# Loading only weight blocks first, first-block passes one chunk apart, and an earlier read of the third sum, in a fused convolution and low-rank kernel on one core

## Chip, cores and metric

The kernel runs on one core of a Trainium2 chip. The metric is the device time of one execution in microseconds (us), as the median of several runs. One execution was also taken with the hardware profiler; all rows shown here are of that one.

## What is computed

The input x has shape 128 x 64 x 1024 (samples, channels, positions). Four residual stages follow one another, each adding its result to x:

```python
x = x + _L0_cond_ref(x, itok_B_8_3872, log_dt, C, log_A_real, A_imag, D)   # masked causal convolution with a state-space kernel
x = x + _L1_cond_ref(x, itok_B_0_15, weights)          # einsum('bct,bcd->bdt', x, weights[condition])
x = x + _L2_cond_ref(x, itok_B_6_15, base_weight, base_bias, lora_A_w, lora_B_w)  # x @ base_weight.T + bias + (x A.T) B.T
x = x + _L3_cond_ref(x, itok_B_0_2, W, lora_A, lora_B_w)  # x @ W.T + 0.5 (x A) B.T
```

Stages 2 and 3 are linear over the 1024 positions, so the kernel first multiplies (base_weight + I) with (W + I) once, and then applies the product to all rows, with the low-rank terms beside it. All arithmetic is float32 with 32-bit sums; matrix products of full precision are made of three passes over a high and a low part of each operand (high x high, high x low, low x high).

## The kernel before

The program is written engine by engine with semaphores. There is no scheduler: on each engine the order is the order of the code. It has three phases.

**Setup (0 to about 179 us).** The SP queue loads the eight 512 KB blocks of W (`w3_raw`, L898) and the eight 512 KB blocks of base_weight (`p2`, L895), and after them the low-rank tables `a3raw`, `b2raw`, `b2raw3` (L909 to L911). Between the first blocks it also loads three small tensors for the convolution kernel (L903) and stores a block of zeros (L906). The ACT queue issues seven more small loads before any of its work (L1111). For each of the eight chunks of W, VectorE adds the identity to the diagonal block (`w3_identity`, L1282), ScalarE makes the high part (`p3[.., 0, ..]`, L1158, semaphore `p3_hi`), and VectorE makes the low part (`p3_low`, L1286, `p3_lo`). The first block of base_weight (`p2[0]`) is split in the same way into `staged[0]`: its high part on ScalarE (L1126, `staged_hi`), its low part on VectorE (L1297, `staged_lo`). The second block (`p2[4]`) gets its identity from GpSimd (L1057), its high part from ScalarE and its low part from VectorE (L1303).

TensorE first runs 20 multiplications by the identity (`keep_clock`, L409), which only keep it busy. Then it computes the product of the first block, the job `d0`, chunk by chunk (L1640 to L1647): for each chunk c of the contraction three passes (a, b), where a picks the high or low part of the staged block and b that of p3; each pass is two multiplications of 512 columns. The job `d4` follows (L1664), then small products with the low-rank table (`a3a`, `a3b`, L1611), and between them four transposes of the parameters of the convolution kernel (`parameters`, L1650 to L1656). The transposes wait for `base_ready`, which VectorE raises at the end of a serial chain of small operations (L1307 to L1373); within the chain it waits for the seven small loads (`in_later`, L1355). The job `a3b` waits until VectorE has copied the transposed parameters (`part_ready`, L1444). The rest of the setup is further products of blocks.

**Convolution (about 179 to 547 us).** For each of the 64 channels TensorE multiplies by a Toeplitz matrix (`convolve`, L1715 to L1748); a hardware loop (`Fori`) runs over groups of eight channels.

**Dense phase (about 547 us to the end).** 32 pairs of samples, one pass of `pair(n, last_one)` for each. Pair 0 and pair 31 are straight code, pairs 1 to 30 are a hardware loop, so that a branch back is taken after pairs 1 to 29. For each pair TensorE computes seven Strassen-like products (L802 to L818), applies low-rank terms (`low_rank`, L825), and, for the next pair, does four quarters of the stage-1 mixing (`quarter`, L787). At the end of a pair's code TensorE has, in this order: the product M7 into the bank `of_p` (`m7_done`), the low-rank terms of the second sample (`v_done`), quarter 3 of the next pair, a wait for `u3_read`, and the last low-rank term into `of_p` (`p_done`). `u3_read` is raised by VectorE once it has read the third sum out of `of_p` (L765), which it may do after `m7_done`. The next pair's code opens with `wide_product` of xa11 (L808, L809 alternating).

VectorE's part at the same place, before the change:

```python
            if not last_one:
                h_low(dve, n + 1, 1)
                sums(n + 1)                      # L680, L681, L684
            dve.wait_ge(m7_done, n + 1)
            tt(y_out[1][:, 0:HB], y_out[1][:, 0:HB], of_p, ALU.add).then_inc(u3_read, 1)   # L765
```

`sums(n + 1)` adds two quarters (L680), makes the low part of xa22 (L681), then waits for ScalarE's high part of that sum (`s1_hi`, L581) and makes the low part xs1 (L684, `s1_lo`), which TensorE needs for the second product of the next pair.

## Time and profile before

| what | value |
|---|---|
| median of 3 runs | 1442.49 us (1442.35 to 1443.65) |
| the profiled execution's own time | 1442.2 us |
| span of its profile | 1440.3 us |
| TensorE (PE) busy | 1430.6 us, 99% of the span |
| VectorE (DVE) busy | 1127.9 us, 78% |
| ScalarE (ACT) busy | 611.8 us, 42% |
| GpSimd (POOL) busy | 101.0 us, 7% |
| moved by DMA | 272.98 MB, mean 190 GB/s |

Times of rows are counted from the start of the span; the profiled execution's own time is 1.9 us more than its span. PE is the matrix multiplications of TensorE, PEld its weight loads, which may run ahead of the multiplications. A matrix multiplication is shown from the start to its modelled end, so neighbours overlap, and a float32 multiplication appears as two records. "Idle before" is how long the engine did nothing ahead of a row, and what ended it.

### The profile page before, as it was taken

How to read it: one execution, taken by the hardware profiler on the slowest of the kernel's cores; microseconds unless marked ns; L12 is line 12 of the kernel's file. 1: busy time of each engine (PE TensorE's matmuls, PEld its weight loads, DVE VectorE, ACT ScalarE, POOL GpSimd, SP SyncE). 2: the span in 40 equal slices, each digit the busy share in tenths (PEclk: the TensorE clock that was granted, in tenths of full speed). 3: DMA queues.
4: the chain of work that ended last, by engine and by line, in shares of the span. 5: the costliest groups of instructions: out<-in, count | busy, mean ns of one | idle time of the engine just before them, and what ended most of it. 6: DMA issues, size and time to landing. Idle time of an engine off the chain costs nothing.

```text
span 1440.3 us, 31112 instructions
## 1 busy us (share of the span) xinstructions
PE 1430.6 (99%) x9274; PEld 1319.5 (92%) x9274; DVE 1127.9 (78%) x2256; ACT 611.8 (42%) x1217; POOL 101.0 (7%) x187
## 2 busy tenths in 40 slices
PE   9999999999999999999999999999999999999999
PEld 7888899999999998999999999999999999999998
DVE  7985398888888887777887787787788788778775
ACT  4331276566656663333433432333343343233332
POOL 2322100000000001000000000000000000000000
PEclk9999999999999999999999999999999999999999
DMA  8032288888888787555565565566556555555642
GB/s 315 1 132 77 59 284 275 272 275 273 275 274 275 271 270 205 189 184 156 176 187 153 171 188 161 154 188 186 155 175 188 156 167 190 160 155 188 185 154 82
DMA packets 117451, 272.98 MB, mean 190 GB/s; under 512 B 24300, under 2 KB 60527, under 8 KB 114759
## 3 DMA queue, kind: packets, MB, share of 16 engines
q1 hardware_dynamic: 107366, 238.91, 53.9%
q10 hardware_dynamic: 10054, 33.68, 5.8%
q8 instruction: 17, 0.28, 0.1%
q14 instruction: 14, 0.11, 0.0%
HBM read 199.60 MB, written 72.88 MB: 189 GB/s over the span
## 4 chain that ended last, share of the span: by engine, by line
PE 98%; DMA 1%; DVE 0%; SPq 0%; issue 0%; DVEq 0%
PE ps L816 18%; PE ps L809 17%; PE ps L1735 14%; PE ps L808 13%; PE ps L787 8%; PE ps L1625 7%; PE ps L1746 6%; PE ps L825 4%; PE ps L1726 3%; PE ps L1611 2%; PE ps L1738 2%; PE ps L1646 1%; PE ps L1634 1%; PE ps L1664 1%; DMA w_raw<-in_L_cond_W 1%; PE ps L800 0%
## 5 line engine op out<-in xcount | busy, mean ns | idle before, releaser
L808 PE MATMUL ps<-weights,xa 128*128 128x256 f32 x1152 | 322.6, 283 | 0.7
L809 PE MATMUL ps<-weights,xa 128*128 128x352 f32 x1152 | 322.2, 321 | 0.0
L816 PE MATMUL ps<-weights,xs 128*128 128x512 f32 x1152 | 292.1, 401 | 0.0
L816 PEld LDWEIGHTS ps<-weights,xs 128*128 128x128 f32 x1152 | 207.1, 189 | 41.3
L574 ACT ACTIVATE a<-ps 128x512 f32<-128x512 f32 x128 | 76.5, 598 | 375.4 <-PE ps L787 375.4
L808 PEld LDWEIGHTS ps<-weights,xa 128*128 128x128 f32 x1152 | 216.8, 188 | 12.4 <-issue 12.3
L1735 PE MATMUL ps<-toep,ut 128*128 128x512 f32 (+2 forms) x1152 | 226.8, 342 | 0.0
L809 PEld LDWEIGHTS ps<-weights,xa 128*128 128x128 f32 x1152 | 216.4, 188 | 0.1
L1735 PEld LDWEIGHTS ps<-toep,ut 128*128 128x128 f32 x1152 | 194.3, 189 | 16.6
L787 PEld LDWEIGHTS ps<-m_gath,x_in 128*128 128x128 f32 x1024 | 130.9, 191 | 7.6 <-DVE x_in L672 2.3
L787 PE MATMUL ps<-m_gath,x_in 128*128 128x128 f32 x1024 | 135.0, 275 | 1.9 <-DVE x_in L672 1.9
L1217 ACT ACTIVATE ut<-xt 128x896 fp32r<-128x896 f32 x64 | 61.0, 954 | 138.3 <-PE ps L1746 129.7
L809 PE MATMUL ps<-weights,xs 128*128 128x352 f32 x384 | 107.7, 322 | 0.0
L662 DVE COPY_PREDICATED x_in<-late,x_nat 128x512 f32<-128x512 uint16 x124 | 92.7, 748 | 18.9 <-DVE late L657 18.7
L1746 PE MATMUL ps<-toep,ut 128*128 128x256 f32 x768 | 107.3, 289 | 0.0
L808 PE MATMUL ps<-weights,xs 128*128 128x256 f32 x384 | 106.4, 280 | 0.0
L384 POOL COPY m_gath<-mix 64x64 f32 x128 | 50.3, 393 | 786.0 <-PE ps L787 709.1
L1625 PE MATMUL ps<-p,staged 128*128 128x512 f32 x432 | 98.8, 390 | 0.0
L1625 PEld LDWEIGHTS ps<-p,staged 128*128 128x128 f32 x432 | 80.9, 188 | 17.9 <-issue 1.1
L1746 PEld LDWEIGHTS ps<-toep,ut 128*128 128x128 f32 x768 | 95.8, 190 | 0.0
L692 DVE COPY hrow<-ps 64x48 f32<-64x48 f32 x128 | 26.3, 205 | 75.1 <-PE ps L809 74.2
L461 ACT ACTIVATE weights<-tab 128x128 fp32r<-128x128 f32 (+1 forms) x256 | 71.6, 353 | 29.4 <-DVE tab L468 29.4
(233 smaller groups left out, 2251.1 us busy)
## 6 DMA issues: line engine op xcount, KB each, us to landing
xt<-in_xt SPq DMA_DIRECT2D x64, 512.0 KB, 5.6
x_d<-yo SPq DMA_DIRECT2D x64, 512.0 KB, 2.9
x_nat<-in_x SPq DMA_DIRECT2D x64, 512.0 KB, 4.2
lags<-kern_d SPq DMA_DIRECT2D x63, 512.0 KB, 4.9
x_in<-x_d SPq DMA_DIRECT2D x62, 512.0 KB
out<-y_out ACTq DMA_DIRECT2D x62, 512.0 KB, 5.3
stack<-b_d SPq DMA_DIRECT2D x130, 128.0 KB, 4.2
tab<-a_d SPq DMA_DIRECT2D x128, 128.0 KB, 2.1
```

The source lines that it names most:

```text
L461: ins = nc.scalar.activation(to, of, ACT.Copy)
L574: ins = copy(raw[:], mixing, ACT.Copy)
L662: nc.vector.copy_predicated(x1_in[v][:, cols], late[:], x_nat[v][:, cols]).then_inc(chosen[v], 1)
L787: ins = mm(acc[:, bank, i * P:(i + 1) * P], x1_in[v][:, c * P:(c + 1) * P], m_gath[v][:], start=True, stop=True)
L808: mm(acc[:, left, 0:HALF], x_part, w[:, 0:HALF], start=start, stop=end, skip_group_check=True)
L809: ins = mm(acc[:, right, 0:HALF + KR], x_part, w[:, HALF:WIDE], start=start, stop=end, skip_group_check=True)
L816: ins = mm(acc[:, bank], operand[:, a, i, :], plain(i, b, m), start=opens and i == a == b == 0, stop=i == K4 - 1 and a == 1, skip_group_ch ...
L825: ins = mm(piece, hs[v][0:rows, j, :], stack[v][0:rows, j, at_col:at_col + width], start=False, stop=j == 1, skip_group_check=True)
L1217: copy(ut[u % 2][:, 0, 0:SPLIT], xt[u % BUFS][:, 0:SPLIT], ACT.Copy).then_inc(ut_hi, 1)
L1625: ins = mm(t[:, cols], staged[n % 2][:, a, c, :], p3[:, c, b, cols], start=c == a == b == 0, stop=c == K8 - 1 and a == 1)
L1735: mm(y[:, half * HB + i * P:(half + 1) * HB], xs[:, a, half * half_t + i, :], tp[:, b, 0:HB - i * P], start=i == a == b == 0, stop=False)
L1746: ins = mm(y[:, to:to + QT], xs[:, a, i, :], tp[:, b, at_col:at_col + QT], start=False, stop=i == half_t - 1 and a == 1)
```

## The change

Three places change. The three small loads of the SP queue and the store of zeros move behind the eight blocks of W (and ahead of `p2[4]`); the seven small loads of the ACT queue move behind ScalarE's last piece of the first two blocks. On TensorE the first pass of chunk c + 1 comes ahead of the second and third pass of chunk c. On VectorE the last third of `sums` becomes `s1_low`, and the read of the third sum (`third`) stands ahead of it.

```diff
@@ VectorE, dense phase
             tt(s1[:], a21[:], a22[:], ALU.add).then_inc(s1_raw, 1)
             tt(xa22[:, 1], a22[:], f(xa22[:, 0]), ALU.subtract).then_inc(a22_lo, 1)
+
+        def third(n):
+            dve.wait_ge(m7_done, n + 1)
+            tt(y_out[1][:, 0:HB], y_out[1][:, 0:HB], of_p, ALU.add).then_inc(u3_read, 1)
+
+        def s1_low(n):
             dve.wait_ge(s1_hi, n + 1)
             dve.wait_ge(s1_raw, n + 1)
             tt(xs1[:, 1], s1[:], f(xs1[:, 0]), ALU.subtract).then_inc(s1_lo, 1)
@@
         sums(0)
+        s1_low(0)
@@
                 sums(n + 1)
-            dve.wait_ge(m7_done, n + 1)
-            tt(y_out[1][:, 0:HB], y_out[1][:, 0:HB], of_p, ALU.add).then_inc(u3_read, 1)
+            third(n)
+            if not last_one:
+                s1_low(n + 1)
@@ SP queue
                     load_p2(p2[0], 0, in_w2[0])
-                if i == 1:
-                    for to, of in ((logs[:, 0:N], log_a_real), (logs[:, N:N + 1], log_dt.unsqueeze(1)), (aim[:], a_imag)):
-                        sp.dma_start(to, of).then_inc(in_small, 16)
-                if i == 2:
-                    sp.wait_ge(consts, 7)
-                    sp.dma_start(kern_d[:, T:T + P], zero[:]).then_inc(kern_stored, 16)
+            for to, of in ((logs[:, 0:N], log_a_real), (logs[:, N:N + 1], log_dt.unsqueeze(1)), (aim[:], a_imag)):
+                sp.dma_start(to, of).then_inc(in_small, 16)
+            sp.wait_ge(consts, 7)
+            sp.dma_start(kern_d[:, T:T + P], zero[:]).then_inc(kern_stored, 16)
             for i in BLOCKS[1:]:
                 load_p2(p2[i], i, in_w2[i])
@@ ACT queue: the loop of seven loads (cri, steps_all, dcol, bias_col, index x3) moves
-            for to, of in (...):
-                act.dma_start(to, of).then_inc(in_later, 16)
...
             stage_high(1)
+            for to, of in (...):
+                act.dma_start(to, of).then_inc(in_later, 16)
             act.wait_ge(trig_in, 1)
@@ TensorE, job d0
+            def first_pass(c, a, b):
+                pe.wait_ge((p3_hi, p3_lo)[b], c + 1)
+                pe.wait_ge((staged_hi, staged_lo)[a], 1)
+                for half in range(2):
+                    cols = slice(half * HB, (half + 1) * HB)
+                    ins = mm(target("d0")[:, cols], staged[0][:, a, c, :], p3[:, c, b, cols],
+                             start=c == a == b == 0, stop=c == K8 - 1 and b == 1)
+                return ins
+
+            first_pass(0, 0, 0)
             for c in range(K8):
-                for a, b in ((0, 0), (1, 0), (0, 1)):
...
+                if c + 1 < K8:
+                    first_pass(c + 1, 0, 0)
+                first_pass(c, 1, 0)
+                ins = first_pass(c, 0, 1)
             ins.then_inc(job_done, 1)
```

TensorE's order at the start of job d0 before the change (the semaphores that a row waits for stand behind it; a row without them is the second half of its pass):

```order
L1646 MATMUL ps<-p_72,staged_73 128x512 [waits staged_hi,p3_hi]
L1646 MATMUL ps<-p_72,staged_73 128x512
L1646 MATMUL ps<-p_72,staged_73 128x512 [waits staged_lo,p3_hi]
L1646 MATMUL ps<-p_72,staged_73 128x512
L1646 MATMUL ps<-p_72,staged_73 128x512 [waits staged_hi,p3_lo]
```

and the same place after it, with numbers in the names (line 1650 is in `first_pass`):

```order
L1650 MATMUL ps<-p3_72,staged0_73 128x512 [waits staged_hi,p3_hi]
L1650 MATMUL ps<-p3_72,staged0_73 128x512
L1650 MATMUL ps<-p3_72,staged0_73 128x512 [waits staged_hi,p3_hi]
L1650 MATMUL ps<-p3_72,staged0_73 128x512
L1650 MATMUL ps<-p3_72,staged0_73 128x512 [waits staged_lo,p3_hi]
L1650 MATMUL ps<-p3_72,staged0_73 128x512
L1650 MATMUL ps<-p3_72,staged0_73 128x512 [waits staged_hi,p3_lo]
```

A second pass that needs only high parts, that of chunk 1, now stands between the first pass of chunk 0 and the two passes of chunk 0 that need a low part.

VectorE's order at the end of a pair of the loop, before:

```order
L680 TENSOR_TENSOR s_170<-a_167,a_168 128x512 [waits quarter_read]
L681 TENSOR_TENSOR xa_159<-a_168,xa_159 128x512
L684 TENSOR_TENSOR xs_157<-s_170,xs_157 128x512 [waits x_s1_raw,x_s1_hi]
L765 TENSOR_TENSOR y_out_172<-y_out_172,ps 128x512 [waits m7_done]
L768 TENSOR_TENSOR y_out_172<-y_out_172,ps 128x512 [waits u3_read,v_done]
L770 TENSOR_TENSOR y_out_172<-y_out_172,ps 128x512 [waits p_done]
```

and after (L685 is the old L765, L690 the old L684):

```order
L680 TENSOR_TENSOR s_170<-a_167,a_168 128x512 [waits quarter_read]
L681 TENSOR_TENSOR xa_159<-a_168,xa_159 128x512
L685 TENSOR_TENSOR y_out_172<-y_out_172,ps 128x512 [waits m7_done]
L690 TENSOR_TENSOR xs_157<-s_170,xs_157 128x512 [waits x_s1_raw,x_s1_hi]
L776 TENSOR_TENSOR y_out_172<-y_out_172,ps 128x512 [waits u3_read,v_done]
L778 TENSOR_TENSOR y_out_172<-y_out_172,ps 128x512 [waits p_done]
```

The read of the third sum and the low part of xs1 have changed places; nothing else moved there.

## Rows read from the trace of the kernel before

**Rows 1.** The page, busy time of each engine over the span.

```profile
PE 1430.6 (99%) x9274; PEld 1319.5 (92%) x9274; DVE 1127.9 (78%) x2256; ACT 611.8 (42%) x1217; POOL 101.0 (7%) x187
```

**Rows 2.** Waits of TensorE's weight loads, whole span: total us, times, longest us.

```profile
PEld ps L808 <- issue: 12.3, 29, 0.5
...
PEld ps L1655 <- DVE lens_cols L1373: 0.3, 1, 0.3
```

**Rows 3.** Timeline of TensorE, start: start us, us, instruction, count, idle before.

```profile
1.57 6.80 PE L409 MATMUL ps<-ident 128*128 128x128 f32 x40 [1.57 <-POOL ident L1021]
8.13 0.70 PE L1646 MATMUL ps<-p,staged 128*128 128x512 f32 x2
10.69 10.99 PE L1646 MATMUL ps<-p,staged 128*128 128x512 f32 x46 [1.85 <-DVE staged L1297]
21.51 11.04 PE L1664 MATMUL ps<-p,staged 128*128 128x512 f32 x48
...
43.46 0.46 PE L1655 MATMUL ps<-ident,par 64*128 64x64 f32 x4
```

**Rows 4.** Timeline of VectorE, the start and its serial chain.

```profile
5.63 0.29 DVE L1293 TENSOR_TENSOR p<-p,ident 128x128 f32<-128x128 f32 x1 [1.18 <-DMA p<-in_L_cond_base_weight]
...
9.11 0.29 DVE L1282 TENSOR_TENSOR w_raw<-w_raw,ident 128x128 f32<-128x128 f32 x1 [0.82 <-DMA w_raw<-in_L_cond_W]
...
11.21 0.29 DVE L1282 TENSOR_TENSOR w_raw<-w_raw,ident 128x128 f32<-128x128 f32 x1 [0.67 <-DMA w_raw<-in_L_cond_W]
...
17.95 0.28 DVE L1282 TENSOR_TENSOR w_raw<-w_raw,ident 128x128 f32<-128x128 f32 x1
...
34.49 2.26 DVE L1345 TENSOR_TENSOR n<-n,n 64x64 f32<-64x64 f32 x1
...
37.37 1.70 DVE L1347 TENSOR_TENSOR n<-n,aim 64x64 f32<-64x64 f32 x1
...
40.87 0.22 DVE L1363 COPY par<-n 64x128 f32<-64x128 f32 x1
```

**Rows 5.** Stretches: length, busy us of PE to POOL, clock, DMA share, GB/s.

```profile
5.00:6.50 1.50, 1.50 (x11) 1.50 (x11) 0.29 (x1) 1.49 (x2) 0.11 (x1) 1.00 0.34 59
...
11.00:19.00 8.00, 8.00 (x35) 6.21 (x34) 7.79 (x12) 6.04 (x6) 0.00 (x0) 1.00 1.03 415
```

**Rows 6.** Timeline of GpSimd: the second block, and beside VectorE's chain.

```profile
19.12 0.57 POOL L1057 TENSOR_TENSOR p<-p,ident 128x128 f32<-128x128 f32 x1 [14.01 <-DMA p<-in_L_cond_base_weight]
...
34.26 4.73 POOL L1053 TENSOR_TENSOR staged<-b2raw,staged 128x1024 fp32r<-128x1024 f32 x2 [6.53 <-ACT staged L1126]
```

**Rows 7.** Timeline of TensorE, end of pair 17, in the loop.

```profile
1047.85 2.99 PE L816 MATMUL ps<-weights,xs 128*128 128x512 f32 x12
...
1051.99 0.72 PE L825 MATMUL ps<-stack,hs 128*128 128x512 f32 x2
...
1052.90 0.32 PE L809 MATMUL ps<-weights,xa 128*128 128x352 f32 x1
```

**Rows 8.** Timeline of TensorE, end of pair 30, which no branch back follows.

```profile
1412.03 0.72 PE L825 MATMUL ps<-stack,hs 128*128 128x512 f32 x2
...
1412.70 0.32 PE L809 MATMUL ps<-weights,xa 128*128 128x352 f32 x1
```

**Rows 9.** Timeline of TensorE in the convolution: first and last of 64 channels.

```profile
179.11 0.88 PE L1726 MATMUL ps<-toep,dt 128*128 128x256 f32 x6
...
541.57 0.88 PE L1726 MATMUL ps<-toep,dt 128*128 128x256 f32 x6
```

**Rows 10.** Timeline of VectorE, end of pair 17.

```profile
1051.26 0.68 DVE L765 TENSOR_TENSOR y_out<-y_out,ps 128x512 f32<-128x512 f32 x1
```

**Rows 11.** Timeline of TensorE's weight loads, end of pair 1.

```profile
609.24 0.30 PEld L825 LDWEIGHTS ps<-stack,hs 128*128 128x128 f32 x2 [0.22 <-DVE y_out L765]
610.05 0.19 PEld L808 LDWEIGHTS ps<-weights,xa 128*128 128x128 f32 x1 [0.52 <-issue]
```

**Rows 12.** DMA issues of the first 60 us: size, median us to landing.

```profile
b2raw<-in_L_cond_lora_B_w SPq DMA_DIRECT2D x1, 512.0 KB, 19.8
```

More of the change, by code:

```diff
@@ L1104, in trig @@
                 nc.scalar.activation(to, to, ACT.Sin, scale=scale, bias=bias).then_inc(fac_sin, 1)
-            for to, of in ((cri[:], ssm_c.rearrange("h n c -> h (n c)")), (steps_all[:], steps.unsqueeze(0).to_broadcast([P, B])),
-                           (dcol[:], ssm_d.unsqueeze(0).to_broadcast([G, C])),
-                           (bias_col[:], bias2),
-                           (index[:, 0:B], cond.unsqueeze(0)), (index[:, B:2 * B], adapter.unsqueeze(0)),
-                           (index[:, 2 * B:3 * B], labeler.unsqueeze(0))):
-                act.dma_start(to, of).then_inc(in_later, 16)
             def stage_high(n):
@@ L1161, in _ @@
             stage_high(1)
+            for to, of in ((cri[:], ssm_c.rearrange("h n c -> h (n c)")), (steps_all[:], steps.unsqueeze(0).to_broadcast([P, B])),
+                           (dcol[:], ssm_d.unsqueeze(0).to_broadcast([G, C])),
+                           (bias_col[:], bias2),
+                           (index[:, 0:B], cond.unsqueeze(0)), (index[:, B:2 * B], adapter.unsqueeze(0)),
+                           (index[:, 2 * B:3 * B], labeler.unsqueeze(0))):
+                act.dma_start(to, of).then_inc(in_later, 16)
             act.wait_ge(trig_in, 1)
@@ L1639, in _ @@
             keep_clock(target("a3a"), FILL_START)
-            for c in range(K8):
-                for a, b in ((0, 0), (1, 0), (0, 1)):
-                    pe.wait_ge((p3_hi, p3_lo)[b], c + 1)
-                    pe.wait_ge((staged_hi, staged_lo)[a], 1)
-                    for half in range(2):
-                        cols = slice(half * HB, (half + 1) * HB)
-                        ins = mm(target("d0")[:, cols], staged[0][:, a, c, :], p3[:, c, b, cols],
-                                 start=c == a == b == 0, stop=c == K8 - 1 and b == 1)
+            def first_pass(c, a, b):
[7 more added lines that the diff above has]
+            first_pass(0, 0, 0)
+            for c in range(K8):
+                if c + 1 < K8:
+                    first_pass(c + 1, 0, 0)
+                first_pass(c, 1, 0)
+                ins = first_pass(c, 0, 1)
             ins.then_inc(job_done, 1)
```

## The prediction

> **What bounds the kernel now.** I read the page first: TensorE is busy for 99% of the span and VectorE for 78% [rows 1]. So only what makes TensorE stand, or start late, can change the time. Three views show where it stands: the waits of its weight loads [rows 2], its timeline at the start [rows 3], and its timeline where one pair of the dense phase ends and the next begins [rows 7, 8]. There are two kinds of place.
>
> At the start TensorE multiplies by the identity until 1.57 + 6.80 = 8.37 us, does one pass of d0, then stands for 1.85 us until the low part of the first block is made [rows 3]. From then on it is fed, except at the parameters: their weight load waits 0.3 us for VectorE [rows 2], so VectorE's chain and TensorE arrive together at 43.46.
>
> In the dense phase the weight load of L808 stands 12.3 us in all, 29 times, put down to "issue" [rows 2]: once for each of the 29 branches back. What it costs the multiplications is read from two ends of pairs. Where the branch follows, the first L809 starts 52.90 - 51.99 = 0.91 us after the last low-rank term [rows 7]; where straight code follows it is 12.70 - 12.03 = 0.67 [rows 8]. That stall is among the smaller: in pair 1 the load stood 0.52 us [rows 11]. The mean stall is 12.3 / 29 = 0.42. The load of pair 17 comes 0.69 us after L825 and stood about 0.39 (L825's two loads take 0.30), for a cost of 0.24, so 0.15 of a stall is hidden, and the mean cost is 0.27 us.
>
> Does a branch by itself cost that? In the convolution, a loop with seven trips round eight channels, 63 steps from channel to channel take 541.57 - 179.11 = 362.46 us, or 5.753 each [rows 9], and no step differs from the next by over 0.01 in the timeline. There the branch is free: no wait that ends late stands near it. In the dense loop one does: `u3_read` stands right before the last two multiplications, and VectorE reads the third sum from 1051.26 to 1051.94, after which L825 starts at 1051.99 [rows 7, 10]. I take it that the issuing side stands at that wait, and only afterwards can issue the last term, branch, and fetch and issue the next pair's code.
>
> **The change part by part.**
>
> *Order of loads.* Nothing is added; eleven small DMAs move. The first blocks of W and base_weight have landed by 5.63, the next block of W only by 9.11 [rows 4], and between 5.0 and 6.5 the DMA engines move 59 GB/s against 415 later [rows 5]: the small loads hold the block up. A 512 KB block at 415 GB/s takes 1.26 us. With only blocks in the queues the third lands at about 5.63 + 1.26 = 6.9; VectorE makes the low part of chunk 0 first; ScalarE's high part of it no longer stands behind seven issues, so that work too is done at about 7.1, and VectorE takes the block then. So VectorE's whole row of work moves by 9.11 - 7.1 = 2.0 us. If the gap in the transfers stays for another reason, the block lands at 8.0 and it moves by 1.1. The three SP loads and the store of zeros now stand ahead of `p2[4]`, as they did; it landed at 19.1 [rows 6] and moves forward with the rest, to about 17 to 18. ScalarE's seven issues come after the high part of that block, when ScalarE would only wait for VectorE, so I cost them at nothing; what uncovers that is a rival below.
>
> *Passes of d0.* The first pass of chunk 1 fills the place where TensorE stood 1.85 us. Its 48 multiplications run at the pace of d4, 11.04 / 48 = 0.23 us [rows 3], so from 8.13 they end at 19.2 instead of 21.51: 2.3 us sooner. For this the high part of chunk c + 1 must be there at 8.8 + 1.38 c; VectorE took a new diagonal block every (17.95 - 11.21) / 5 = 1.35 us [rows 4], a little less than the 1.38 that six multiplications take, and ScalarE's part follows each within some 1.3 us: 8.4 for chunk 1, where 8.8 is needed, and no step later than that. With the block at 8.0 TensorE loses another 0.6.
>
> *What is late next.* TensorE would be at the parameters at 43.46 - 2.3 = 41.1. VectorE's chain starts 2.0 us sooner, but it meets GpSimd's two operations of 2.4 us each, beginning at 34.26 [rows 6]. Two operations of VectorE that otherwise take 0.22 lasted 2.26 and 1.70 beside them: 3.5 us lost [rows 4]. In the new order GpSimd finds VectorE some eight operations further on, past the reciprocal that ran beside it, so I expect 4.2 us lost. The chain then ends at 43.4 - 2.0 + 0.7 = 42.1 and TensorE waits there one us. The copy that `a3b` waits for hangs on the same chain and moves with it. **The start gives 43.4 - 42.1 = 1.3 us.** Bounds: 2.0 (no additional time lost to GpSimd) and 0.6 (block at 8.0). After that TensorE's work is in turn what the other engines wait for, and its stretches have no stall, so the gain is carried to the end.
>
> *The third sum.* M7 ends at 1047.85 + 2.99 = 1050.84 [rows 7], and VectorE, which now reads the sum before making the low part of xs1, can begin at about 1050.88 in place of 1051.26 [rows 10]: `u3_read` comes 0.38 us sooner. A load of L808 that stood 0.42 us on average then stands 0.04, and the longest stands 0.14, below the 0.15 that is hidden. **29 x 0.27 = 7.8 us.** Bounds: nothing (the branch is not held by this wait) and 7.8 plus the few hundredths by which L825 itself may come sooner, at most 28 x 0.02 = 0.6. In pairs 0 and 1 VectorE is later than in the others and L825 itself waits, 0.22 us in pair 1 [rows 11] and less in pair 0: another 0.3. The low part of xs1 comes 0.7 us later, at 1052.1; its product follows 24 multiplications after 1052.7, over 3 us later, so that cover holds. In the last pair nothing stood ahead of the read, and nothing changes.
>
> **Sum:** 1.3 + 7.8 + 0.3 = 9.4 us off the profiled execution's 1442.2, so 1432.8; the median of the runs is 0.3 higher, so **1433.0** rounded.
>
> **The rivals.**
>
> *The branch is not held by the wait.* The issuing side might put the waiting multiplication in a queue and read on; then the 0.4 us are the price of the branch whatever VectorE does, and the change gives 1.3 + 0.3: 1440.6. Against it stand the convolution's free branches [rows 9], and pair 1: its L825 came 0.22 us late, and the next load followed 0.81 us after it, not sooner than the 0.69 of pair 17 [rows 11, 7], so the delay was passed on rather than absorbed. For it: I see the issuing side in no row, and 0.81 beside 0.69 is also in the spread from pair to pair. The Trainium skill speaks for this rival ("Advanced Engine Details and Errata", Sequencer Loop): an engine instruction is pushed into the engine's queue, waits for its semaphores there, and further ones are read meanwhile. By that rule the third part gives 0.3 us instead of 8.1. I give it 0.2.
>
> *Half of it.* The wait holds the branch, but freed 0.38 us earlier the issuing side still has to wait for room, and half of each stall stays: 3.9 in place of 7.8, so 1436.7. I give it 0.13.
>
> *The seven loads come late.* They are issued from about 19 to 23 us, while big loads fill the DMA engines; the last of these took 19.8 us to land [rows 12]. If the small ones took 20.2 from the last issue, VectorE would get them at 43.6, where it needed them at 40.87 [rows 4], and the chain would end 2.7 us later than before. With a branch that the wait does not hold, the time is 1442.2 + 2.7 - 0.3 = 1444.6, and more with each further us of landing. It decides from a landing at 40.9. Against it: the big loads are all down by about 35 us, and what is issued beside them should not take longer. I give it 0.03.
>
> **How the numbers follow.** My forecast has 0.62: 1431.2 to 1435.0, from 1.3 widened to 0.6 to 2.0 at the start, and 7.0 to 8.4 at the branches. The half has 0.13, the rule's case 0.2, the late loads 0.03, and 0.02 is left for what I do not see. The range reaches from the low end of my own case to the rule's case: **1431.2 to 1441.0**. A change of 0.2% (2.9 us) is about what a measurement of this kernel can tell from none. My case and the half are faster by more: 0.75. The rule's case, 1.6 us, is within it: with the rest, 0.22. Slower by more: 0.03.
>
> **What would show it.** In the changed kernel's profile d0's 48 multiplications run from 8.1 without a stall and d4 starts near 19.2; the second W block's diagonal is made near 7.1; the parameters start near 42.1, with their load waiting about 1 us for VectorE. In the waits the row of L808's loads put down to issue shrinks from 12.3 us to under 4; ends of pairs in the loop have L809 about 0.67 us after L825; the step from pair to pair is shorter by 0.27 us. If that row stays at 12 us I am wrong about what holds the branch; if L1655 starts at 43.4 again, the start gave nothing.

## The result and the profile after

| | before | after |
|---|---|---|
| median of 6 runs each | 1442.42 us (1442.22 to 1443.65) | 1430.62 us (1429.81 to 1432.42) |
| ratio, with its 95% interval | | 0.9919 (0.9906 to 0.9932) |
| the profiled execution's own time | 1442.2 us | 1431.91 us |
| span of its profile | 1440.3 us | 1430.0 us |

The kernel is 11.8 us faster by the medians and 10.3 us by the two profiled executions. Forecast were 9.4 us and 1433.0, with 1431.2 as the low end: direction and place were right, the sum was too small, and the result lies 0.6 us below the range.

**Page.** Busy time of each engine over the span, after:

```profile
PE 1421.1 (99%) x9274; PEld 1318.3 (92%) x9274; DVE 1124.2 (79%) x2256; ACT 612.4 (43%) x1217; POOL 106.7 (7%) x187
```

The counts are those of [rows 1]: no work was removed. The matrix multiplications' busy time fell by 9.5 us, although the weight loads' fell by only 1.2, because the timeline leaves no gap between multiplications there: in before, at the end of pair 17, L825 is drawn from 1051.99 to 1052.71 and L808 from 1052.68, although the load between them stood 0.39 us. So a share of 99% said little about how much could be gained, before and after.

**Waits of TensorE's weight loads,** after (total us, times, longest us):

```profile
PEld ps L795 <- DVE x_in L672: 3.5, 2, 2.9
...
PEld ps L816 <- issue: 1.4, 6, 0.4
...
PEld ps L1667 <- DVE lens_cols L1378: 0.9, 1, 0.9
```

The row of 12.3 us, 29 times [rows 2] has become 1.4 us, 6 times (the old L808 is L816). The row counts only stalls above 0.15 us. With the smaller ones these 29 loads stood 2.9 us in the trace, at least 0.04 each, which is also what the one at the end of pair 30 has, where no branch follows. The wait at the parameters has grown from 0.3 to 0.9 us, as forecast. The largest is now one at the entry of the dense phase; it had stood second in the list of before as well:

```profile
PEld ps L787 <- DVE x_in L672: 2.3, 2, 1.9
```

**End of pair 17,** timeline of TensorE's multiplications after (start us, us, instruction, count):

```profile
1042.26 3.00 PE L824 MATMUL ps<-weights,xs 128*128 128x512 f32 x12
1045.09 0.64 PE L833 MATMUL ps<-stack,hs 128*128 128x256 f32 x4
1045.56 1.06 PE L795 MATMUL ps<-m_gath,x_in 128*128 128x128 f32 x8
1046.37 0.71 PE L833 MATMUL ps<-stack,hs 128*128 128x512 f32 x2
1046.93 0.28 PE L816 MATMUL ps<-weights,xa 128*128 128x256 f32 x1
1047.04 0.33 PE L817 MATMUL ps<-weights,xa 128*128 128x352 f32 x1
```

and VectorE at the same place:

```profile
1045.29 0.69 DVE L685 TENSOR_TENSOR y_out<-y_out,ps 128x512 f32<-128x512 f32 x1 [0.34 <-PE ps L824]
1045.89 0.69 DVE L690 TENSOR_TENSOR xs<-s,xs 128x512 fp32r<-128x512 f32 x1
```

VectorE now waits for M7, reads the third sum from 1045.29 to 1045.98, and only then makes the low part of xs1. L833 (the old L825) starts at 1046.37, so 0.39 us after the read; before, it started 0.05 us after it [rows 7, 10]. The first L817 follows L833 by 1047.04 - 1046.37 = 0.67 us, the distance that straight code had [rows 8]. Over all pairs of the loop that distance was 0.85 to 1.04 us before and is 0.66 to 0.70 now, with one exception: pair 1, where it is 0.93. The timeline of the weight loads shows that one:

```profile
608.84 0.30 PEld L833 LDWEIGHTS ps<-stack,hs 128*128 128x128 f32 x2
609.55 0.19 PEld L816 LDWEIGHTS ps<-weights,xa 128*128 128x128 f32 x1 [0.41 <-issue]
```

VectorE's timeline shows why this one is left:

```profile
608.11 0.68 DVE L685 TENSOR_TENSOR y_out<-y_out,ps 128x512 f32<-128x512 f32 x1
```

The read did not wait for M7 here, as in pair 17; it followed VectorE's earlier work without a gap and ended at 608.79, 0.05 us before L833. So in pair 1 the wait still ended late, and its stall stayed. In `third_alone` and `pool_waits`, two kernels described below, VectorE was in time in pair 1 too: the read ended 0.40 us ahead of L833, and the first L817 came 0.66 and 0.67 us after it.

**The issuing side in the trace.** The timeline does not draw what an engine's sequencer does, but the view of one line does (PEldq is TensorE's sequencer, L374 is the loop; the numbers are the shortest, median and longest duration in ns, and the start). The branch back at the end of pair 17, before:

```profile
L374 PEldq COMPARE_BRANCH  x1: 215/215/215, 1052.1 to 1052.1; - x1
```

and after:

```profile
L374 PEldq COMPARE_BRANCH  x1: 208/208/208, 1046.1 to 1046.1; - x1
```

In the trace's finer times it starts 0.15 us after the end of VectorE's read (1051.94 and 1045.98), in each of the 29 taken branches of before and of after. Where TensorE's own work stands makes no difference to it: in before it starts 0.10 us after the last low-rank term, in after 0.25 us ahead of it, while quarter 3 still runs. A taken branch lasts 0.21 to 0.22 us. The first load of the next trip then starts 0.78 us after the end of the read on average in before (0.69 to 0.87), and 0.76 in after (0.71 to 0.86). So the issuing side does stand at the wait for `u3_read`, and from there the next trip's first load takes much the same stretch in both kernels, about 0.8 us. What of this stretch TensorE's last work does not cover is the stall.

**Start,** timeline of TensorE after:

```profile
1.57 6.99 PE L409 MATMUL ps<-ident 128*128 128x128 f32 x40 [1.57 <-POOL ident L1027]
8.32 11.43 PE L1650 MATMUL ps<-p,staged 128*128 128x512 f32 x48
19.63 11.17 PE L1676 MATMUL ps<-p,staged 128*128 128x512 f32 x48
30.64 11.03 PE L1616 MATMUL ps<-a3raw,p 128*128 128x160 f32 x80
42.37 0.46 PE L1667 MATMUL ps<-ident,par 64*128 64x64 f32 x4 [0.70 <-DVE lens_cols L1378]
```

d0 runs without a stall and d4 starts at 19.63 instead of 21.51 [rows 3]. The parameters start at 42.37 instead of 43.46, after a wait for VectorE: 1.1 us, where 1.3 were forecast. What the DMA engines did between 5.0 and 6.5 us (length, busy us of PE to POOL, clock, DMA share, GB/s):

```profile
5.00:6.50 1.50, 1.50 (x9) 1.50 (x9) 1.19 (x2) 1.42 (x2) 0.11 (x1) 1.00 0.95 358
```

They moved 358 GB/s instead of 59 [rows 5], so the gap in the transfers was the small loads' doing. Which of the two queues' loads did it was not separated. Still the next block of W was not taken at 7.1 as forecast but at 7.49, as VectorE's timeline shows:

```profile
5.31 0.29 DVE L1298 TENSOR_TENSOR p<-p,ident 128x128 f32<-128x128 f32 x1 [0.85 <-DMA p<-in_L_cond_base_weight]
5.58 1.23 DVE L1291 TENSOR_TENSOR p<-w_raw,p 128x1024 fp32r<-128x1024 f32 x1
7.49 0.29 DVE L1287 TENSOR_TENSOR w_raw<-w_raw,ident 128x128 f32<-128x128 f32 x1 [0.69 <-DMA w_raw<-in_L_cond_W]
7.70 1.22 DVE L1302 TENSOR_TENSOR staged<-p,staged 128x1024 fp32r<-128x1024 f32 x1
...
15.73 2.44 DVE L1291 TENSOR_TENSOR p<-w_raw,p 128x1024 fp32r<-128x1024 f32 x2
19.61 1.35 DVE L1308 TENSOR_TENSOR staged<-p,staged 128x1024 fp32r<-128x1024 f32 x1 [1.45 <-ACT staged L1125]
...
33.79 2.13 DVE L1352 TENSOR_TENSOR n<-n,aim 64x64 f32<-64x64 f32 x1
35.96 2.28 DVE L1353 TENSOR_TENSOR n<-n,exps 64x64 f32<-64x64 f32 x1
```

The low part that d0 needs (L1302) now runs from 7.70 to 8.92, where before TensorE had to wait for it until 10.69 [rows 3]. Beside GpSimd's work two operations of VectorE took 2.13 and 2.28 us instead of 0.22: 4.0 us lost, where 4.2 were forecast and 3.5 had been lost before. New is the idle time of 1.45 us ahead of L1308, at 19.61. The timeline of GpSimd and that of ScalarE show where it comes from:

```profile
16.95 1.54 POOL L1063 TENSOR_TENSOR p<-p,ident 128x128 f32<-128x128 f32 x1 [11.82 <-DMA p<-in_L_cond_base_weight]
```

```profile
18.52 1.06 ACT L1125 ACTIVATE staged<-p 128x1024 fp32r<-128x1024 f32 x1 [1.61 <-POOL p L1063]
```

The second block now lands at 16.95 instead of 19.12 [rows 6]. But GpSimd's addition of the identity, which took 0.57 us there, takes 1.54 now. ScalarE has to wait 1.61 us for it, and VectorE waits for ScalarE. It ends at 18.49, 0.32 us after VectorE's last two low parts of W, which end at 15.73 + 2.44 = 18.17. The nine profiles with moved loads fall into two kinds. In five (both of after among them) the addition took 1.16 to 1.54 us and ended 0.31 to 0.32 us after VectorE's pair, and the parameters started at 42.25 to 43.47. In the other four it took 0.46 us, VectorE's pair took 2.67 to 2.74 instead of 2.44 or 2.45, and the parameters started at 41.79 to 42.80. So one of the two holds the other, and which it is hangs on the moment at which the block lands. VectorE's second operation of the pair starts about 1.21 us after its first. In the four, GpSimd's addition started 1.12 to 1.20 us after the pair's start, so just ahead of that second operation; in the five, 1.21 to 1.60 us after it.

**Where the 10.3 us of the profile lie.** For both kernels I took TensorE's timeline and split each of the 30 steps from pair to pair at the first multiplication of every group. The means, in us; the other eleven groups together differ by less than 0.01:

| segment | before | after | times 30 |
|---|---|---|---|
| last low-rank term to the next pair's first multiplication | 0.717 | 0.553 | 4.9 |
| M1, the 24 weight loads behind it | 3.427 | 3.313 | 3.4 |
| quarter 3 to the last low-rank term | 0.840 | 0.812 | 0.8 |
| M5 | 3.320 | 3.301 | 0.6 |
| M2 and M4 | 6.664 | 6.641 | 0.7 |
| whole step | 27.681 | 27.340 | 10.2 |

So all of it lies in the dense phase. The 1.1 us of the start are not in the profiled execution's total, because both kernels start the dense phase at 550.52 us. After was there sooner, but its first quarter waited for a part of x that comes back from memory:

```profile
PE ps L795 <- DVE x_in L672: 3.1, 2, 2.8
```

In before and in the eleven other profiles of this study the longest wait of this row was between 0.6 and 2.3 us. What the start gives therefore shows in the medians and not in this one execution; its own time is also 1.3 us above the median of after. Over all profiles of this study it is seen at this place too: the dense phase starts at 548.2 to 550.5 us in the nine with moved loads (mean 549.4) and at 550.5 to 552.7 in the four without (mean 551.4).

### The profile page after: what moved, and what is told of

Its sections match the earlier page's. It is cut to its first block, busy times and chain, and to the rows that moved or that the text cites. A ratio compares the mean times of both kernels' runs of the same rounds, so it can differ in the third digit from the quotient of the medians.

```text
span 1430.0 us, 31112 instructions
## 1 busy us (share of the span) xinstructions
PE 1421.1 (99%) x9274; PEld 1318.3 (92%) x9274; DVE 1124.2 (79%) x2256; ACT 612.4 (43%) x1217; POOL 106.7 (7%) x187
## 4 chain that ended last, share of the span: by engine, by line
PE 96%; DVE 2%; DMA 1%; SPq 1%; issue 0%; POOL 0%; ACT 0%; DVEq 0%; POOLq 0%
PE ps L824 19%; PE ps L817 17%; PE ps L1747 14%; PE ps L816 13%; PE ps L795 8%; PE ps L1630 7%; PE ps L1758 6%; PE ps L833 4%; PE ps L1738 3%; PE ps L1750 2%; PE ps L1616 1%; PE ps L1639 1%; DMA p<-in_L_cond_base_weight 1%; PE ps L808 0%; DMA x_in<-yo 0%; SPq L906 0%
## 5 line engine op out<-in xcount | busy, mean ns | idle before, releaser
L817 PE MATMUL ps<-weights,xa 128*128 128x352 f32 x1152 | 321.0, 322 | 0.0
L816 PE MATMUL ps<-weights,xa 128*128 128x256 f32 x1152 | 318.5, 279 | 0.0
L816 PEld LDWEIGHTS ps<-weights,xa 128*128 128x128 f32 x1152 | 217.0, 188 | 3.0 <-issue 1.4
L817 PEld LDWEIGHTS ps<-weights,xa 128*128 128x128 f32 x1152 | 216.1, 188 | 0.6
L384 POOL COPY m_gath<-mix 64x64 f32 x128 | 56.1, 439 | 772.2 <-PE ps L795 693.6
L817 PE MATMUL ps<-weights,xs 128*128 128x352 f32 x384 | 107.2, 321 | 0.0
L816 PE MATMUL ps<-weights,xs 128*128 128x256 f32 x384 | 105.9, 279 | 0.0
```

The lines of the kernel that those rows point to most:

```text
L816: mm(acc[:, left, 0:HALF], x_part, w[:, 0:HALF], start=start, stop=end, skip_group_check=True)
L817: ins = mm(acc[:, right, 0:HALF + KR], x_part, w[:, HALF:WIDE], start=start, stop=end, skip_group_check=True)
```

## The experiments

Two theories stood against each other. **Held:** the issuing side of TensorE stands at `u3_read` before it can issue the last term and branch back. **Not held:** the branch costs 0.4 us whatever VectorE does. For the start the question was which of the two edits gives anything. Each kernel of a batch was timed beside runs of before on the same chip; those had medians of 1442.75, 1442.39 and 1443.39 us in the three batches. The ratios are of these comparisons and can differ from the quotient of two medians by some 0.0005.

### One part alone

`third_alone` is before with only VectorE's edit:

```diff
+            third(n)
+            if not last_one:
+                s1_low(n + 1)
-            dve.wait_ge(m7_done, n + 1)
-            tt(y_out[1][:, 0:HB], ...).then_inc(u3_read, 1)
```

> The kernel before, with only VectorE's read of the third sum moved ahead of the low part of xs1. Theory A (the branch back is held by the wait for u3_read): the stall of L808's weight load falls from 12.3 us to under 2, a step from pair to pair goes from 27.68 to 27.34 us, as in the changed kernel, and the time falls by 10 to 10.6 us (ratio 0.9928), although the start is untouched. Rival B (the branch is not held, the gain of the changed kernel comes from a different start): 0 to 1 us. Rival C (each part needs the others): between, 3 to 8 us.

Measured: 1433.08 us, ratio 0.9929 (0.9915 to 0.9942). Its list of waits is headed by the start's:

```profile
PEld ps L1654 <- ACT p L1166: 2.4, 1, 2.4
...
PEld ps L816 <- issue: 1.6, 9, 0.2
```

and the stall behind the branch is as small as in after; the step from pair to pair is 27.323 us. This edit alone is worth 9.7 us by the medians and 10.2 by the ratio, most of the whole. A branch that costs the same whatever VectorE does cannot give that.

`loads_alone` is before with only the small loads moved:

```diff
-                if i == 1:
-                    ... logs, logs, aim
-                if i == 2:
-                    ... kern_d
+            ... logs, logs, aim, kern_d      (behind the eight blocks of W)
-            ... seven loads of the ACT queue
             stage_high(1)
+            ... seven loads of the ACT queue
```

> The kernel before, with only the small loads moved behind the weight blocks. My theory: the second W block lands near 7.5 in place of 9.1, the chain of VectorE ends at 42.3 in place of 43.4, the first low part is ready at 8.9 so TensorE stands only some 0.5 us after its filling, and the parameters start at 42.4, where VectorE's chain is what is waited for. Gain at 43.46: 1.1 us, with or without the new order of passes. Rival (the passes are needed for it): under 0.5 us.

Measured: 1441.11 us, ratio 0.999 (0.9981 to 0.9999). Two rows of it, TensorE's timeline at the start and the wait behind the branch:

```profile
8.58 11.52 PE L1643 MATMUL ps<-p,staged 128*128 128x512 f32 x48
```

```profile
PEld ps L808 <- issue: 11.9, 29, 0.5
```

The stall behind the branch is untouched. But d0 already runs without its gap, in the old order of passes.

`passes_alone` is before with only the order of the passes of d0:

```diff
+            first_pass(0, 0, 0)
             for c in range(K8):
+                if c + 1 < K8:
+                    first_pass(c + 1, 0, 0)
+                first_pass(c, 1, 0)
+                ins = first_pass(c, 0, 1)
```

> The kernel before, with only the passes of d0 one chunk apart. The second pass of TensorE would need the high part of chunk 1, made at 9.4 to 10.5 from the block that lands at 9.1, so TensorE stands as long as before, and VectorE's chain still ends at 43.4: no change within 0.2 us. If the order of passes were worth something by itself, d4 would start before 21.3.

Measured: 1442.43 us, ratio 0.9995 (0.9986 to 1.0004), no difference. The first pass of chunk 1 has nothing to work on while the block is late; it waits 1.77 us for ScalarE's part of that block, and another pass 0.35 us:

```profile
10.59 1.74 PE L1645 MATMUL ps<-p,staged 128*128 128x512 f32 x6 [1.77 <-ACT p L1158]
```

In this profile the parameters start at 45.01, where I had expected 43.4 to 43.5. `third_alone`, with the start of before unchanged, has 44.77, so the spread between executions reaches as far, and no price of the passes can be read from it.

`loads_and_passes` is after without VectorE's edit (both diffs above).

> The changed kernel without the early read of the third sum. My theory: as loads_alone, 1.1 us off at the parameters; d4 starts at 19.6, but that is lost again while TensorE waits for VectorE's chain. L808's stall stays near 12.3 us and the step from pair to pair at 27.68. Time 1441.3. Rival (the passes keep what they gain): another 0.5 us or more below loads_alone.

Measured: 1440.82 us, ratio 0.9984 (0.9975 to 0.9994). In its profile the parameters start at 41.83 and the step is 27.703 us, as before. Beside `loads_alone` the difference is 0.3 us, within both intervals.

`no_passes` is after with the old order of the passes (the diff of `passes_alone` the other way round).

> The changed kernel with the old order of passes in d0. If the passes are worth nothing by themselves, as VectorE's chain is what is waited for at the parameters, the time is that of the changed kernel within 0.5 us (1430.6) and the parameters start near 42.4. If they are worth what they gain in d0, it is slower by 0.5 us or more.

Measured: 1432.23 us, ratio 0.9919 (0.9905 to 0.9932), the same ratio as after. Its d0 has a gap of 0.34 us:

```profile
9.62 10.69 PE L1651 MATMUL ps<-p,staged 128*128 128x512 f32 x46 [0.34 <-DVE staged L1302]
```

So in this execution the order of the passes had 0.3 us left to fill, and even that is lost in the wait at the parameters. They start at 43.47, where I had expected 42.4. The ratio alone could not show 0.3 us: its interval is 1.9 us to either side.

`after_again` is after, unchanged, for one more profile.

> The changed kernel once more, unchanged, for a second profile: the dense phase takes the same time from its first product to the end within 0.5 us, and what differs between the two executions lies in the landing of the W block (7.5 in the first) and in the wait for the last rows before the dense phase (2.8 us in the first, 1.7 in the kernel before). Expected: a shorter wait there, 1 to 2 us, and a span 1 us below 1430.0.

Measured: one time, 1431.95 us. Its start differs from that of the first profile:

```profile
9.56 10.81 PE L1650 MATMUL ps<-p,staged 128*128 128x512 f32 x46 [0.50 <-ACT p L1157]
...
43.44 0.46 PE L1667 MATMUL ps<-ident,par 64*128 64x64 f32 x4 [1.14 <-DVE lens_cols L1378]
```

Here the parameters start at 43.44, no sooner than before, because the second W block was taken at 8.12 instead of 7.49. The step (27.346 us) repeats; the row of the stall reads 2.5 us, 12 times, since more of the small stalls are above 0.15 us (with all of them 3.6 us beside 2.9). Over the nine profiles with moved loads the block was taken between 7.49 and 8.31 and the parameters started between 41.79 and 43.47; in the four without, 9.11 to 9.22 and 43.46 to 45.01. The start's gain is a spread: on average the parameters start at 42.5 in the nine and 44.2 in the four, 1.7 us apart, while the profile from which I forecast 1.3 was the earliest of the four.

### Is it the wait or the branch?

`third_after_v` is after with one wait more: VectorE may read the third sum only after `v_done`, which TensorE raises just before quarter 3. The place in VectorE's order stays that of after.

```diff
         def third(n):
             dve.wait_ge(m7_done, n + 1)
+            dve.wait_ge(v_done, n + 1)
```

> The changed kernel, order of VectorE unchanged, but its read of the third sum also waits for v_done, so that u3_read comes some 0.5 us later than in the changed kernel (about 0.1 later than before the change). Theory A (time of u3_read holds the branch): L808's stall is back at 12 us or more, L825's successor starts late, the gain of the third part is gone: 10 to 14 us slower than the changed kernel, 1441 to 1445. Rival B (what helped is that the low part of xs1 comes after the read, not when the read ends): the time stays within 2 us of the changed kernel.

Measured: 1448.34 us, ratio 1.0034 (1.0021 to 1.0046). Its wait behind the branch:

```profile
PEld ps L817 <- issue: 12.2, 29, 0.5
```

The stall is back at its old size, although everything else of the change is in. The kernel lost 17.7 us to after, more than I had expected, because L834 itself now waits as well: quarter 3 to the last term takes 1.012 us instead of 0.812, 6.0 us over 30 pairs. The stall takes (0.715 + 3.408) - (0.553 + 3.313) = 0.257 per pair, 7.7 us. M2 with M4 has (6.730 - 6.641) x 30 = 2.7 of the rest, and 1.2 us more lie in pair 0. VectorE's read and L834 at the end of a pair show the wait with no slack again, as in before:

```profile
1055.17 0.69 DVE L686 TENSOR_TENSOR y_out<-y_out,ps 128x512 f32<-128x512 f32 x1 [0.88 <-PE ps L834]
```

```profile
1055.91 0.73 PE L834 MATMUL ps<-stack,hs 128*128 128x512 f32 x2
```

The read ends at 1055.86 and L834 starts 0.05 us after it. The branch back again starts 0.15 us after the read, in all 29 places.

`third_dose` is after with two fills of 64 columns of unused PSUM before the read. They compute nothing that is used, and make `u3_read` later by a little:

```diff
             dve.wait_ge(m7_done, n + 1)
+            for i in range(2):
+                nc.vector.memset(acc[:, SMALL_BANK, (2 + i) * P:(2 + i) * P + 64], 0.0)
             tt(y_out[1][:, 0:HB], ...).then_inc(u3_read, 1)
```

> The changed kernel, with two small fills of unused columns of the sums' memory on VectorE between its wait for m7_done and its read of the third sum, so that u3_read comes some 0.2 to 0.3 us later than in the changed kernel and still before the place where the kernel before had it (0.4 later). They compute nothing that is used. Theory A with the hidden part: each 0.1 us of delay adds 0.1 us to the weight load of L808 once it is past what is hidden, so its stall reads 4 to 8 us in all where the changed kernel has 1.4 and the kernel before 12.3, and the time is 0.5 to 4 us above the changed kernel. A step (all or nothing) would give either 1.4 or 12.

Measured: 1434.2 us, ratio 0.9934 (0.992 to 0.9947). VectorE at the end of pair 17, and the wait behind the branch:

```profile
1046.45 0.19 DVE L686 MEMSET ps<- 128x64 f32 x2 [0.39 <-PE ps L826]
1046.55 0.67 DVE L687 TENSOR_TENSOR y_out<-y_out,ps 128x512 f32<-128x512 f32 x1
```

```profile
PEld ps L818 <- issue: 6.4, 23, 0.5
```

```profile
L374 PEldq COMPARE_BRANCH  x1: 208/208/208, 1047.4 to 1047.4; - x1
```

The read ends at 1047.22, and L835 starts at 1047.49: 0.27 us later, where before it was 0.05 and in after 0.39. These values line up with the stalls: 0.05 and 12.3 us in before, 0.05 and 12.2 in `third_after_v`, 0.27 and 6.4 here, 0.39 and 1.4 in after. The last term to L819 takes 0.75 us on average over the 31 ends of pairs, between the 0.93 of before and the 0.68 of after. It is no mixture of full stalls and none: outside pair 1 every branch of this kernel has a stall of 0.14 to 0.32 us, where before has 0.34 to 0.52 and after 0.04 to 0.19. The branch starts 0.15 us after the read here too. So the stall is graded by how late the wait ends, and a slack of about 0.4 us is what makes it nearly go away. By the ratios this kernel is 2.2 us slower than after, though the two intervals overlap. This also answers the rival in which half of the stall stays: with the slack whole, L817 follows L833 as in straight code.

`before_two_pairs` keeps everything of before, but TensorE's loop has 15 trips of two pairs, so half of the branches are gone:

```diff
-        over_pairs(pe, pair)
+        pair(0, False)
+        with pe.Fori(1, PAIRS // 2) as k:
+            pair(2 * k - 1, False)
+            pair(2 * k, False)
+        pair(PAIRS - 1, True)
```

> The kernel before, with TensorE's loop over pairs 1 to 30 written as 15 trips of two pairs, so half of its branches back are gone; all else, VectorE's order too, unchanged. Theory A (the stall is the branch held behind a late wait): the stall of L808 appears 14 or 15 times, 6 us in place of 12.3, and the time falls by 4 to 5 us. Rival D (the stall comes from the late wait alone, with or without a branch): 29 stalls, no change. Rival B (a branch costs 0.4 us whatever the wait): the same halving as theory A, told apart from it by the next run.

Measured: 1439.5 us, ratio 0.9977 (0.9966 to 0.9987). The wait, and two ends of pairs that follow each other, without a branch and with one:

```profile
PEld ps L808 <- issue: 7.4, 14, 0.7
```

```profile
1050.82 0.73 PE L825 MATMUL ps<-stack,hs 128*128 128x512 f32 x2
1051.39 0.28 PE L808 MATMUL ps<-weights,xa 128*128 128x256 f32 x1
...
1078.16 0.72 PE L825 MATMUL ps<-stack,hs 128*128 128x512 f32 x2
1078.94 0.38 PE L808 MATMUL ps<-weights,xa 128*128 128x256 f32 x1
```

Of the 31 ends of pairs 17 have L809 0.67 to 0.69 us after L825, the other 14 have 0.95 to 1.17. So a late wait without a branch behind it makes no stall. The 14 stalls are longer than before (7.4 / 14 = 0.53 us instead of 0.42), which is why only 3 us were gained and not the 4 to 5 that I had expected. The additional 0.1 us lies behind the branch: from its end to the first load it is 0.52 us on average here and 0.41 in before. Why a loop body of twice the length makes this longer stays open.

`after_two_pairs` is the same edit on after.

> The changed kernel with the same 15 trips of two pairs on TensorE. Theory A: hardly a stall is left to halve (1.4 us in 6 places), so under 0.7 us faster. Rival B (each branch costs by itself): the gain of before_two_pairs shows again, 4 to 5 us.

Measured: 1431.65 us, ratio 0.9919 (0.9906 to 0.9933): no difference from after, and a step of 27.353. Where the wait ends in time, fewer branches gain nothing. Late wait and branch are both needed for the full stall, and taking either away removes most or all of it. The longer body shows here as well: with the same slack of 0.40 us its row reads 2.5 us, 10 times, and behind some of its 14 branches L817 comes 0.74 to 0.83 us after L833.

### The wait that is left at the start

`pool_waits` is after, with GpSimd's two operations of the chain's time held back until the chain is done:

```diff
+            pool.wait_ge(base_ready, 1)
             stage_low(2)
             stage_low(3)
```

> The changed kernel, with GpSimd waiting for base_ready before its two low parts of 2.4 us each. My theory: they no longer stop VectorE's two operations (2.1 and 2.3 us where 0.2 is usual), VectorE's chain ends near 38.2 in place of 42.3, TensorE no longer waits 0.7 us at the parameters, which then start at 41.7, and the time falls by 0.7 us. GpSimd's parts are done by 43, long before TensorE's b2_0 at 51. Rival (VectorE's stretched operations are not GpSimd's doing): chain still ends at 42.3, no change.

Measured: 1430.55 us, ratio 0.9911 (0.9898 to 0.9925). VectorE's reciprocal and the two operations behind it, and the end of its chain:

```profile
34.01 0.55 DVE L1352 RECIPROCAL n<-n 64x64 f32<-64x64 f32 x1
34.59 0.22 DVE L1353 TENSOR_TENSOR n<-n,aim 64x64 f32<-64x64 f32 x1
34.84 0.22 DVE L1354 TENSOR_TENSOR n<-n,exps 64x64 f32<-64x64 f32 x1
...
38.74 0.39 DVE L1379 CAST lens_cols<-steps_all 64x64 f32<-64x64 int32 x2
```

The operations that lasted 2.13 and 2.28 us take 0.22 each, the chain ends at 39.1 instead of 42.3, and TensorE no longer waits at the parameters. It starts them at 42.25, though, since in this execution its own work got there no sooner: d0 had lost 0.63 us waiting for ScalarE. The time cannot be told from that of after. Its interval reaches furthest down of all kernels here, but I would not claim a gain over after.

## Where the prediction was right, and the step that failed

**Order of loads.** The mechanism was right: the gap in the transfers went (59 to 358 GB/s) and the block came earlier. It was mis-sized: taken at 7.1, measured 7.49 to 8.31 over nine profiles, so my bound of 8.0 is nearer to the truth than my value. I had timed a 512 KB block at the full 415 GB/s in queues that hold only blocks. After's window shows 358, by which the block takes 1.46 us; what makes up the rest of the delay stays open.

**Passes of d0.** I wrote that they fill the 1.85 us and did not ask what they would be worth without the loads, or the loads without them. The runs say: the passes alone nothing (0.9995), their absence from after nothing (0.9919 beside 0.9919). Once the block comes at 7.5 to 8.3, VectorE's low part is ready at 8.9 to 9.7 and the stall is 0.0 to 0.6 us in either order. The 2.3 us that the paragraph on the passes counts are the loads' doing.

**What is late next.** Right in kind: VectorE's chain takes over as the bound, the loss to GpSimd came to 4.0 us (forecast 4.2), and the wait at the parameters was 0.70 us on the multiplications (forecast one). What I missed is the other direction: GpSimd's small addition at 16.95 was slowed itself, 1.54 us instead of 0.57, and cost the chain 1.45 us. Its ends 0.3 us behind VectorE's pair in five profiles speak for a hold by VectorE, and the longer pair in the other four for a short hold by GpSimd; no run took either away. The Trainium skill's page "SBUF — State Buffer" (Who interferes with whom) has both: an operation of VectorE with two inputs in SBUF and one of GpSimd that reads SBUF hold each other up, and which one loses is decided by which was issued first. `pool_waits` agrees for the first direction, with 2.13 and 2.28 us against 0.22; the second is only read from those rows.

**The start as a whole.** Forecast 1.3 us, in bounds of 0.6 to 2.0. The two kernels without VectorE's edit give 1.4 us (ratio 0.999) and 2.3 us (ratio 0.9984), each with an interval of about 1.4 us to either side. The after of the profile had 1.1 at the parameters, and lost it again at the entry of the dense phase. "The gain is carried to the end" was argued too quickly: the wait for x_in at 550 us, the second largest row of before's waits, takes up or gives back about a microsecond from one execution to the next, and the prediction did not price it. In the sum of the medians, 11.8 us less the 10.2 of the dense phase leave 1.6 for the start.

**The third sum.** The reason was right, and it was the step that carried the forecast. `third_alone` shows the gain, `third_after_v` brings the stall back, `third_dose` grades it, and the two kernels with two pairs per trip show that it takes both the late wait and the branch. The issuing side, which the prediction saw in no row, is in the trace: its branch starts 0.15 us after VectorE's read in all eleven profiles with one pair per trip. The rival of the branch that is not held, with its 0.2, is refuted. So is the half, with its 0.13. The convolution, whose branches the prediction took as free, bears it out: its six taken branches last 0.21 to 0.24 us each, and its steps are all 5.75 us long. The seven late loads never happened: in no profile did the chain wait for them. (Its own sum gives 23 + 20.2 = 43.2 for their landing, not 43.6.)

The Trainium skill's rule ("Advanced Engine Details and Errata", Sequencer Loop) says that an instruction is pushed into its engine's queue and waits for its semaphores there, and that other ones can be read and queued while a control instruction is being executed. The prediction read it as letting the issuing side go past a wait. The trace does not agree with that at this place: the branch, which stands behind two multiplications that wait for `u3_read`, starts 0.15 us after the read, whether that is before or behind TensorE's start on them. It does agree in that the issuing side runs ahead of multiplications that wait for nothing but the engine: in after, 0.25 us ahead of L833.

**The step that failed is the size of the sum for the dense phase,** a main term a little too small and two further terms put at nothing. I forecast 7.8 + 0.3 = 8.1 us there and measured 10.2:

| term | forecast | measured (table of segments) |
|---|---|---|
| stalls behind the branch | 29 x 0.27 = 7.8 | 4.9 + 3.4 = 8.3 |
| pair 1's own wait | 0.3 | 0.3 |
| L825 itself sooner in the other pairs | 0, bound 0.6 | 0.8 - 0.3 = 0.5 |
| M5, and M2 with M4 | not priced | 0.6 + 0.7 = 1.3 |

The four measured terms come to 10.4; the other eleven groups give 0.2 back. The main term was good to 0.5 us, although one stall fewer than counted went away (that of pair 1): the other 28 were worth 8.3 / 28 = 0.30 us each, not 0.27. L825 started within 0.05 us of the end of VectorE's read in before, which meant that it was itself held a little in every pair; I saw that, bounded it at 0.6, and then took 0 where the row spoke for the bound. The last line I had not priced at all. Its two halves differ. M5 takes 3.291 to 3.312 us in the eight kernels with VectorE's new order, `third_after_v` among them, and 3.315 to 3.328 in the five with the old one, so its 0.6 us goes with that order; why stays open. M2 with M4 takes 6.61 to 6.73 us over all the kernels of this study, without order by edit, so its 0.7 may be the spread between executions, and no run settles it. Finally the range. Its low end had 2.0 at the start, 8.4 at the branches (the 0.6 for L825 is in it) and 0.3 in pairs 0 and 1. Off the median of 1442.5 that is 1431.8; the recorded 1431.2 is 0.6 lower without a term for it, and in the same way the forecast itself comes to 1433.1 and not 1433.0. Nothing stood in it for gains outside the three places that I had looked at. The 1.3 us of the table's last line would have taken the low end to 1430.5 and held the result.

## What to carry to other kernels

Look at the last wait ahead of a loop's branch back. If it ends just as the engine needs it, the wait costs more than its row shows, since the next trip's first weight loads come late. Let the releaser do its part about 0.4 us sooner (here 0.7% of the time), or put two trips in one body (0.2%). What the sequencer does is in the trace of its own line: compare the start of the branch with the end of the work that releases the wait. And price two edits at the same place separately and together: here the earlier loads alone removed the stall that the new order of passes was meant to fill.

## What the runs showed of the hardware that I had not expected

A late wait two multiplications ahead of a branch and the branch itself (0.21 us) show no stall singly and 0.42 us of stalled weight load together. The branch starts 0.15 us after the work that ends the wait, and the next trip's first load 0.7 to 0.9 us after it, wherever the engine's own work stands. A loop body of double length makes this stretch 0.1 us longer, and each stall with it. And GpSimd's addition of 128 x 128, in some executions 0.46 us and in others 1.54, held back ScalarE by 1.6 us and VectorE by 1.4 when it started 1.21 us or more after VectorE's pair of operations; when it started up to 1.20 us after it, it lasted 0.46 us and VectorE's pair 0.3 us longer.
